# Attention: ScalarE copies the next chunk's K out of its bank ahead of the logarithm of the denominator

## The reference

```
def _time_interp(x, eps):            # curr: one step back, prev: one step ahead
    return eps * curr + (1.0 - eps) * prev
R = _time_interp(x, EPS_R) @ Wr.T + br
K = _time_interp(x, EPS_K) @ Wk.T + bk
V = _time_interp(x, EPS_V) @ Wv.T + bv
e  = exp(clip(-w * t_rem + K, -20, 10))
eu = exp(clip(U + K, -20, 10))
A = shift(cumsum(e * V)) + eu * V
B = shift(cumsum(e)) + eu
out = (sigmoid(R) * (A / B)) @ Wo.T + bo
```

## Time and profile before

| | us |
|---|---|
| median of 3 runs | 1374.68 (1374.64 to 1377.61) |
| the profiled execution | 1377.34 |
| its span, first to last instruction | 1375.3 |
| PE busy | 1327.4 (97% of the span) |
| DVE busy | 1090.5 (79%) |
| ScalarE busy | 813.5 (59%) |
| POOL busy | 634.0 (46%) |
| mean granted TensorE clock | 0.996 |

### The profile page before, as it was taken

The page is one execution under the profiler, slowest core; times in us unless marked ns, Lnnn a source line. Parts: engine busy times, 40 slices in busy tenths (PEclk is TensorE's granted clock), DMA queues, the critical chain, the costliest instruction groups (busy, mean ns, idle before and its releaser), DMA issues. The chain is left out here.

```text
span 1375.3 us, 19352 instructions
## 1 busy us (share of the span) xinstructions
PE 1327.4 (97%) x6330; PEld 1098.3 (80%) x6330; DVE 1090.5 (79%) x1782; ACT 813.5 (59%) x1555; POOL 634.0 (46%) x558
## 2 busy tenths in 40 slices
PE   5899999999999999999999999999999899999998
PEld 4777887887888878878886778888888778888886
DVE  6999989889899898898988776655555677777774
ACT  5875666656666666666665464444446366666664
POOL 4665344343443433434434544444445455555552
PEclk9999999999999999999999999999999999999999
DMA  9010101001001010010050354444443312222212
GB/s 349 9 30 2 61 31 50 13 31 61 13 17 61 31 58 3 31 61 0 1 222 1 138 210 168 150 146 153 166 147 120 104 59 92 91 91 91 92 62 92
DMA packets 54539, 113.92 MB, mean 83 GB/s; under 512 B 2768, under 2 KB 7120, under 8 KB 52560
## 3 DMA queue, kind: packets, MB, share of 16 engines
q1 hardware_dynamic: 54480, 113.22, 23.2%
HBM read 88.05 MB, written 25.17 MB: 82 GB/s over the span
## 5 line engine op out<-in xcount | busy, mean ns | idle before, releaser
L818 POOL TENSOR_TENSOR a_ss<-a_ss,a_eu 128x512 f32<-128x512 f32 x64 | 82.7, 1293 | 281.4 <-DVE a_ss L630 281.4
L612 DVE SCALAR_TENSOR_TENSOR bank<-bank,k_or_row 128x510 f32<-128x510 f32 x192 | 132.8, 692 | 56.3 <-ACT k_or_row L494 53.3
L823 POOL TENSOR_TENSOR a_sv<-a_sv,a_euv 128x512 f32<-128x512 f32 x64 | 82.8, 1294 | 119.0 <-DVE a_sv L647 119.0
L494 ACT ACTIVATE k_or_row<-bank 128x512 f32<-128x512 f32 x192 | 113.8, 593 | 5.7 <-PE bank L82 0.5
L514 ACT ACTIVATE bank<-bank,a_nbr 128x510 f32<-128x510 f32 x64 | 42.3, 661 | 123.0 <-DVE bank L612 123.0
L401 PE MATMUL bank<-a_wo_hi,a_y_hi 128*128 128x512 f32 x256 | 100.4, 392 | 0.0
L401 PE MATMUL bank<-a_wo_hi,a_y_lo 128*128 128x512 f32 x256 | 99.7, 389 | 0.0
L401 PE MATMUL bank<-a_wo_lo,a_y_hi 128*128 128x512 f32 x256 | 99.6, 389 | 0.0
L1510 POOL TENSOR_TENSOR b_cx_lo<-b_cx,b_cx_hi 128x512 fp32r<-128x512 f32 x32 | 40.6, 1299 | 113.2 <-ACT b_cx_hi L1205 113.2
L827 POOL TENSOR_TENSOR a_y_lo<-a_yy,a_y_hi 128x512 fp32r<-128x512 f32 x64 | 85.6, 1337 | 3.6 <-ACT a_y_hi L537 3.6
L526 ACT ACTIVATE bank<-a_ss 128x512 f32<-128x512 f32 x64 | 38.7, 604 | 74.8 <-DVE a_ss L653 74.8
(11 more groups left out here) (246 smaller groups left out, 4719.4 us busy)
## 6 DMA issues: line engine op xcount, KB each, us to landing
xres<-in_x SPq DMA_DIRECT2D x8, 1024.0 KB, 5.3
x_after_attention<-xres SPq DMA_DIRECT2D x8, 1024.0 KB, 4.3
xin<-x_after_attention SPq DMA_DIRECT2D x8, 1024.0 KB, 5.6
b_ct<-in_ctx_t SPq DMA_DIRECT2D x8, 1024.0 KB, 6.5
b_cx<-in_ctx SPq DMA_DIRECT2D x8, 1024.0 KB, 7.7
xres<-x_after_attention SPq DMA_DIRECT2D x8, 1024.0 KB, 5.7
x_after_cross<-xres SPq DMA_DIRECT2D x8, 1024.0 KB, 4.4
xin<-x_after_cross SPq DMA_DIRECT2D x8, 1024.0 KB, 5.5
```

What stands on the lines that cost most here:

```text
L494: sc.activation(u3[:, :, 1:], ps[m][:, :, :], ACT.Copy, scale=MIX[m]).then_inc(left[m], 1)
L612: ve.scalar_tensor_tensor(out=ps[m][:, :, 0:T - 1], in0=ps[m][:, :, 1:T], scalar=1.0 - MIX[m], in1=u3[:, :, 0:T - 1], op0=ALU.mult, op1=AL ...
L818: gp.tensor_tensor(ss3[:, :, 0:T], ss3[:, :, 0:T], eu[:, :, :], ALU.add).then_inc(b_done, 1)
L823: gp.tensor_tensor(sv3[:, :, 0:T], sv3[:, :, 0:T], euv[:, :, :], ALU.add).then_inc(a_done, 1)
```

## The change

`leave("k", g + 1)`, ScalarE's copy of the next chunk's K, is issued at the end of chunk g, behind `exp_r` and the copy of the turned x and ahead of `log_d`; before, it was the first instruction of chunk g+1, behind `log_d`. Only the very first chunk still copies its K at its start. In the last chunk of the last tile there is no next K.

```
                     g = i * HC + c
                     back = c > 0 or not is_first(i)
                     ahead = not is_last(i)
-                    leave("k", g)
+                    if not back:
+                        leave("k", 0)
                     if back:
                         first_reciprocal(g - 1)
                     edge("k", g, edge_k)
...
                     k = c - 3
                     if 0 <= k < KC and ahead:
                         xt_high(i + 1, 1 - par, k)
+                    if ahead or c < HC - 1:
+                        leave("k", g + 1)
+                    if 0 <= k < KC and ahead:
                         log_d(g, (i + 1) * KC + k + 1)
                     else:
                         log_d(g, 0)
```

## The result

The changed kernel takes **1367.15 us** (median of 4 runs, 1366.33 to 1367.27), the kernel before 1375.93 beside it (4 runs, 1374.64 to 1377.61): ratio 0.9935, 95% interval 0.9922 to 0.9947. That is faster by 0.65%, 8.8 us, with 1366.0 forecast. The forecast took its 8.7 us off 1374.68, a median of three executions; taken off 1375.93 they give 1367.2. Lines behind the edit have higher numbers in the changed kernel: `weigh` is L646 (was L642), `mix` L616 (L612), `denominator` L657 (L653), the quotient L664 (L660).

What follows compares the result with a forecast made beforehand. DVE's chain sets the tile, with PE's 89.0 us the floor close under it. Tiles 2, 4, 6 (4.3), 3 and 5 (3.4), 0 (0.4) and 7 (0.6) sum to 8.7 us off 1374.68: 1366.0, range 1361.5 to 1370.0.

Steps and rivals of the forecast that it cites:

- The saving of 0.43 a boundary: From one chunk to the next, the quotient starts 0.43 us sooner, though 1.19 us of DVE's idling before the mix goes.
- t: End of DVE's `denominator`; the quotient was to move from 1.79 us after it to 1.36 us after it.
- Where it counts: Gain behind chunks 2 to 7 only; none behind chunks 0 and 1, at the loop's jump, or in most of tile 0.
- the two covered boundaries: Behind chunks 0 and 1: four statistics (2.46 us) or four residual subtractions outlast the exponential, so nothing is saved.
- the loop's jump: Start of tiles 3 and 5: DVE's mix starts 2.06 us late through DVE's own sequencer, so nothing is saved.
- The lead and its limit: How far `weigh` ends ahead of PE's need; above 1.23 us (2.05 in turn chunks) K's end delays the logarithm.
- The sum: Tiles 2, 4, 6 give 4.3 us, tiles 3 and 5 3.4, tile 0 0.4, tile 7 0.6: 8.7 us.
- the cover by POOL: Tile 0, chunks 2 to 6: DVE's clip ends 0.29 us after POOL's last split, so coming 0.43 sooner gains nothing.
- the end of tile 7: PE's 1.89 us idling before L409, behind DVE, shrinks as DVE's lead grows: 0.7 us, of which 0.6 was counted.
- K comes late: Rival, chance 0.04: a late K holds the copy and the logarithm, up to 0.6 us worse a boundary, 1381 us.
- What would show it: Signs in the later profile: mix hardly idles, quotient by t + 1.4 in chunks 4 to 6, tile 4 about 89.4 us.
- The clock: Rival, chance 0.17: a shorter wait at attention's end no longer brings on the 1.2 GHz stretch; 1.5 us more, 1364.5.

Runs made afterwards that it cites:

- the exponential in four: The changed kernel with the exponential behind the logarithm issued as four instructions of 128 columns each: 1380.61 us, ratio 1.0039 to the kernel before.

## Why the prediction was right

**The saving of 0.43 a boundary.** Right: the quotient moved from t + 1.79 to t + 1.36, and with the exponential lengthened to put it back, the gain was gone.

**Where it counts.** Right: with the new order at the two covered boundaries alone nothing came, with it at the other six all of it. At the loop's jump the step held, too, and the run without a loop shows that it is DVE's own sequencer.

**The lead and its limit.** Right, nearly to the digit. Behind tile 4's chunk 6 `weigh` ends at 460.09 + 0.74 and PE starts V at 463.21, a lead of 2.38 (forecast 2.26). The leads behind tile 3's chunk 7 and tile 4's chunks 0 and 1 were 1.89, 1.89 and 0.59 (1.94, 1.95, 0.67). Then PE loses 0.29 (V starts 11.17 apart for 10.88) and, a chunk later, 0.14 more (11.49 for 11.35): 0.43 in all, where 0.15 was worked out and 0.35 put down. The 0.2 put on top for a hand-over had no row. No part of the wait is fixed: with two statistics moved all of it went. The lead behind chunk 6:

```profile
460.09 0.74 DVE L646 SCALAR_TENSOR_TENSOR a_ee<-bank,a_col,a_ee 128x512 f32<-128x512 f32 x1
```

```profile
463.21 0.39 PE L80 MATMUL bank<-a_xt_hi,a_wv_hi 128*128 128x512 f32 x1
```

Earlier K lifted the limit and the wait went.

**The sum.** Tiles 2, 4 and 6 gave 1.41, 1.41 and 1.40 (1.4 each). Tiles 3 and 5 gave 1.71 and 1.91 (1.7 each). Tiles 0 and 1 gave 0.53 (0.4). In tile 0 the cover by POOL held: in chunk 4 the clip starts 0.19 behind POOL's last split, where it started 0.61 behind it, and lasts 1.38 instead of 0.97, so it ends 0.28 behind the split's end, as it did before (0.29):

```profile
72.72 1.38 DVE L628 TENSOR_SCALAR a_eu<-a_eu 128x512 f32<-128x512 f32 x1
```

What tiles 0 and 1 gave comes from two boundaries, not one: behind tile 0's chunk 6 the next `weigh` comes after 11.00 instead of 11.43, and behind its chunk 7 after 12.31 instead of 12.60; up to there the changed kernel stood 0.17 later. Tile 7 gave 0.79 up to L409 (0.6). Together that is 9.2 against 8.7, and 8.8 by the medians.

**One term had the right size for a reason that was only half right.** For the end of tile 7 the step took the higher lead there as the work of the new order in that tile. The old order there brings L409 another 0.59 forward: the gain comes from the lead with which DVE enters tile 7, and the new order spends part of it, since K is late there. The same holds behind chunk 7 of tiles 1, 3 and 5, which costs the even tile that follows 0.29 each time. The rival *K comes late* was thus at work, at a few boundaries and at 0.26 each (t + 2.05 for t + 1.79), too small to turn the sign.

**What would show it.** Not all of the signs came as named. The mix idles hardly at all behind chunks 2 to 4; behind 5, 6 and 7 it idles 0.25, 0.55 and 0.88, and the quotient idles 0.49. By its own words the prediction was wrong if the quotient started later than t + 1.4 in chunks 4 to 6; it starts at t + 1.37 behind chunk 4, but at t + 1.44 and t + 1.74 behind 5 and 6. Behind chunk 5 the logarithm waits for the copy, too, by not quite 0.1, which was another sign of being wrong. The list of signs left out what the sum had in it: the leads there, 2.08 and 2.38, lie above the limit of 2.05, and the quotient is late by 0.08 and 0.38, about as much as they exceed it.

**The clock.** In the profiled execution the stretch at 0.50 behind PE's wait is not there, and what that rival put at 1.5 us measured 1.70. Its reason does not hold: with the exponential in four the wait is 2.00, longer than before, and the eight matmuls behind it take 3.67 all the same.

```profile
748.83 3.67 PE L409 MATMUL bank<-b_raw_wk,bwide 128*128 128x512 f32 x8 [2.00 <-DVE a_ee L624]
```

Of the thirteen profiles, the kernel before has the only one with 5.37 at this place. Some 72 us behind L409, ahead of a product of the cross attention, PE waits 1.9 to 2.4 us in all thirteen; a stretch at 0.50 stands behind that wait in five of them, the kernel before and the changed one not among these. So a wait of that length is not enough to bring the stretch on, and one profile of each kernel does not show that the change took it away; what decides stays open. For the medians, 8.8 apart with 9.2 explained by the tiles, it isn't needed.

## What to carry to other kernels

When a wait is taken out, ask which operation the waiting engine needs next and when that is ready: the gain is the move of that later start, here 0.43 of 1.19. Write down lead and lag chunk by chunk; a gain counts only until the lead meets the next limit, and beyond that limit an in-order engine that now waits for the other input loses, so the new order can be right at some boundaries and wrong at others. An idle time that comes back once in a loop and is released by nothing is worth a look at the loop's own jump.

## What the runs showed of the hardware

A jump back in a loop costs little or some 2 us, and the length of an engine's program seems to take part in it. ScalarE starts its next instruction 0.25 us behind the branch in the changed kernel, whose loop has 376 instructions of ScalarE between two jumps in the trace, and 2.5 us behind it with the exponential in four, at 424. DVE needs 2.8 us at 353. So length alone does not decide, and where the code lies was not varied.

The Trainium skill (Runtime: NRT & Kernel Launch, "Instruction fetch mechanics") says that a taken branch whose target is not in the current window of two pages of instructions has to wait for a fetch. The slow jumps, 2.05 of idling for DVE and 2.07 for ScalarE, agree with that in kind, and both vanish in straight code; no run here shows where the pages lie.
